# Sequence layer with a scan in blocks: where the decay from a token to later blocks is made (sums first, exponential in token order, one transposition), on one core

## The chip, the core and the metric

One core of a Trainium2 chip. The metric is the device time of one execution in microseconds (us). Of the core's engines five matter here: TensorE (matrix products and transpositions, results to PSUM), VectorE, ScalarE and GpSimd (element by element), and the queues that issue transfers. In the profile they are PE (PEld for its weight loads), DVE, ACT, POOL and SP.

## The reference

Two sequences of 2048 tokens with 256 features. A normalisation, then a state space layer with 512 inner channels and 16 states, then a second normalisation and a feed-forward layer with butterfly weights, each added to its input. The change concerns the scan:

```
delta = softplus(x_dbl[..., 0]);  B = x_dbl[..., 1:17];  C = x_dbl[..., 17:33]
A = -exp(A_log)
step:  h = h * exp(delta_t * A) + x_t * (delta_t * B_t)
       y_t = einsum('dn,n->d', h, C_t)
```

## The kernel before

Time runs in four tiles of 512 tokens (index k), each in four groups of 128 tokens (index c), each group in eight blocks of 16 (index j). Both sequences ("batch" b = 0 and 1) go through a tile one after the other. The scan is written as products: inside a block token by token ("diagonal"), from a token to later blocks of its group ("off diagonal"), and from group to group through a state of 16 x 512.

For the off-diagonal part each token's B needs its decay up to the start of every later block. The kernel before makes it so. `softplus` (L1380) gives `delta` per token and `dB` = delta times B, with tokens on the partitions. GpSimd's `weigh_gaps` (L560) spreads rate times `before_block` times delta over 128 columns (8 blocks x 16 states) for each group: `gap_w`. TensorE's `gap_products` (L768) multiplies it with the matrix `after`, which sums over later tokens and transposes at once. ScalarE's `exp_gaps` (L1099) takes the exponential out of PSUM into `b_hat`. Beside that, GpSimd's `mask_b` (L542) spreads `dB` in token order (`bd_tok`), TensorE transposes it (`decayed_b`, L877), and VectorE's `weigh_b` (L1437) multiplies the two. `off_diagonal` (L810) then forms the product of `b_hat` and `c_hat`.

Each engine runs its list of instructions in a fixed order, written out by hand in `first_half` and `second_half` (the names occur once for each engine); semaphores tie the engines together. PSUM tiles are dealt out in a ring of three wide and three small banks by `WIDE_ORDER` and `SMALL_ORDER` (L60 to L75): a use waits until the use three places earlier in its list has been read. The second half of one tile and the first half of the next stand in one loop; the first half of tile 1 stands ahead of it, with the preparation of the weights between its steps.

The order around the change, in the first half, batch 0: VectorE runs `softplus`, a convolution (three steps, `convolve`, L1342), `take_sums` (L1406), a convolution, `weigh` (L1424), `weigh_b`, a convolution, two `diagonal_times_c` (L1464), a convolution, `sum_diagonal`, `assemble`, `advance_state` and four `gate`s (L1488). GpSimd runs `place_c`, `weigh_gaps`, `mask_b`, `diagonal_gaps` (L550), `place_c_block` (L568) and `diagonal_times_b` (L577). ScalarE runs `exp_sums`, `copy_z`, `exp_gaps`, `copy_z`, `exp_diagonal`, `take_c_start`, `take_c_block`, `copy_z`, `copy_first_state`, then `silu_x` of batch 1 (behind a table load). TensorE runs `step_sums` (L756), a projection, `decayed_b`, a projection, `decayed_c_start`, `spread_c`, `decayed_c_block`, a projection, `off_diagonal`, `state_inputs` (L787), `x_projection` of batch 1 (L731) and `ssm_output` (L820), which writes the tiles that the gates read.

In batch 1 VectorE's order is `softplus`, `first_residual`, `second_stats`, `take_sums`, `weigh`, `second_normalise` (L1512, four `tensor_scalar` steps of L1255), `weigh_b`, `low_parts`; GpSimd's is `mask_b`, `rstd_of`, `diagonal_gaps`, `place_c_block`, and, from the second half, `residual_with_bias` (L582). TensorE transposes the normalised tile (`ln2T`, L709), then `c_start` and `cbd`, then runs `state_inputs` and the feed-forward products.

Of the kernel before, what the change touches and what calls it, by code (L numbers as in the profile page):

```python
# [30 lines left out]
ALU = mybir.AluOpType  # L31
# [3 lines left out]
P = 128  # L35
# [4 lines left out]
NS = 16  # L40
# [81 lines left out]
def bass_preln_ssm_butterfly_ffn(  # L122
# [4 lines left out]
    with ctx:  # L127
# [40 lines left out]
        rate_before = sb("rate_before", [P, NB, NS])  # L168
# [15 lines left out]
        delta = sb("delta", [P, GR])  # L184
# [64 lines left out]
        def mark_read(ins, name, i, b):  # L249
# [21 lines left out]
        gap_w_ready = Signal(sem("gap_w_ready"), 1)  # L271
        c_placed = Signal(sem("c_placed"), 1)
        bd_ready = Signal(sem("bd_ready"), 1)
        sums_ready = Signal(sem("sums_ready"), 1)
# [21 lines left out]
                     gaps_ready, diag_summed, c_start_ready, c_block_ready, b_end_ready, states_ready, gated, hid_ready]  # L296
        by_scalar = [halo_moved, xi_copied, xc_ready, z_ready, exp_ready, decays_ready, group_decay_ready, diag_exp,
                     first_state, halo_saved, hid_high]
        by_pool = [rstd1, rstd2, c_placed, gap_w_ready, bd_ready, diag_gaps, cbd_ready, diag_times_b, x1b_ready]
# [177 lines left out]
        def _(pool):  # L477
# [64 lines left out]
            def mask_b(k, b):  # L542
# [6 lines left out]
                                   ALU.mult).then_inc(bd_ready.handle, 1)  # L549
# [9 lines left out]

            def weigh_gaps(k, b):  # L560

                pool.wait_ge(dB_ready.handle, dB_ready.value(k, b, 1))
                written(pool, k, "gap", 0, b, ago=1)
                pool.tensor_tensor(gap_w[:, :, :, :].rearrange("p c j n -> p c (j n)"),
                                   rate_before[:, :, :].rearrange(flat).unsqueeze(1).to_broadcast([P, GR, P]),
                                   delta[:, :].unsqueeze(2).to_broadcast([P, GR, P]), ALU.mult)\
                    .then_inc(gap_w_ready.handle, 1)
# [21 lines left out]
            def first_half(k):  # L589
                place_c(k, 0)  # L590
                weigh_gaps(k, 0)
                mask_b(k, 0)
                diagonal_gaps(k, 0)
                place_c_block(k, 0)
                diagonal_times_b(k, 0)
                place_c(k, 1)
                weigh_gaps(k, 1)
                mask_b(k, 1)
                rstd_of(k, 0, BATCH, var2, rstd2)
                diagonal_gaps(k, 1)  # L600
                place_c_block(k, 1)

# [18 lines left out]
        def _(pe):  # L621
# [134 lines left out]
            def step_sums(k, b):  # L756
# [5 lines left out]
                for n, mask in enumerate((upto, block_upto, after)):  # L762
                    pe.matmul(bank[:, n * GR:(n + 1) * GR], mask[:, :], delta[:, :], start=True, stop=True)
                pe.matmul(bank[:, 12:13], dA[:, :, :].rearrange(flat), ones[:, 0:1], start=True, stop=True)
                mark_written(pe.matmul(bank[:, 16:16 + GR * BL], in_block[:, :], d_place[:, :, :].rearrange(flat),
                                       start=True, stop=True), "sums", 0, b)

            def gap_products(k, b):  # L768

                bank = tile_of("gap", 0, b)  # L770
                free(pe, k, "gap", 0, b)
                pe.wait_ge(gap_w_ready.handle, gap_w_ready.value(k, b, 1))
                for c in range(GR):
                    last = pe.matmul(bank[:, c * P:(c + 1) * P], gap_w[:, c, :, :].rearrange(flat), after[:, :],
                                     start=True, stop=True)
# [888 lines left out]
```

## Time and profile before

| | |
|---|---|
| time, median of 3 runs | 631.44 us (630.95 to 631.99) |
| the profiled execution | 632.72 us, its span 630.8 us |
| TensorE busy (PE) | 560.5 us, 89% of the span |
| VectorE busy (DVE) | 443.5 us, 70% |
| ScalarE busy (ACT) | 303.1 us, 48% |
| GpSimd busy (POOL) | 123.9 us, 20% |
| granted TensorE clock, mean | 0.951 of 2.4 GHz |

A busy share is an average over stages with different limits, and TensorE's busy time counts products that overlap in its pipeline. What a stage waits for is read from its own stretch: from the waits in brackets in the timeline, and from the chain of work that ended last.

### The profile page before, as it was taken

The numbers are of one execution on the slowest core, as the hardware profiler recorded it, in microseconds if no ns is written. First come the engines' busy times: TensorE is split into PE (matmuls) and PEld (weight loads), VectorE is DVE, ScalarE is ACT, GpSimd is POOL, SyncE is SP. The second block draws the span as 40 slices with busy tenths as digits, with TensorE's granted clock in tenths as the row PEclk, the third lists the DMA queues.
The fourth block names the chain that finished last, engine by engine and source line by source line (L and its number), as shares of the span: only waits on it lengthen the run. The fifth ranks groups of instructions, "written<-read, shape, count | busy, mean of one in ns | idle before, by whom it ended". The sixth has DMA issues, their size and how long they took to land.

```text
span 630.8 us, 8980 instructions
## 1 busy us (share of the span) xinstructions
PE 560.5 (89%) x2996; PEld 436.9 (69%) x2996; DVE 443.5 (70%) x883; ACT 303.1 (48%) x511; POOL 123.9 (20%) x104
## 2 busy tenths in 40 slices
PE   4989776679999997979999989979999988979996
PEld 3747345647899773747899665847899664848895
DVE  5748868876556789877556699887555699977432
ACT  3655739146055766044144866054254865162252
POOL 4213100240012032250021042250020041340010
PEclk9988876899999999979999998979999999979999
DMA  8332020010010100010000000000100000000000
GB/s 239 4 22 4 0 66 2 1 35 2 3 64 2 34 1 2 0 34 0 33 33 0 33 0 0 0 33 0 33 33 0 33 0 0 0 0 2 0 34 34
DMA packets 33067, 12.88 MB, mean 20 GB/s; under 512 B 22003, under 2 KB 32499, under 8 KB 33044
## 3 DMA queue, kind: packets, MB, share of 16 engines
q1 hardware_dynamic: 31444, 9.96, 7.3%
q10 hardware_dynamic: 1600, 2.62, 1.2%
q8 instruction: 13, 0.21, 0.2%
q14 instruction: 10, 0.08, 0.0%
HBM read 8.39 MB, written 4.19 MB: 20 GB/s over the span
## 4 chain that ended last, share of the span: by engine, by line
PE 58%; DVE 23%; ACT 8%; issue 7%; DMA 2%; POOL 1%; DVEq 0%; ACTq 0%; POOLq 0%
PE acc L869 14%; PE wide L858 12%; PE wide L727 8%; DVE xc L1346 6%; PE wide L847 4%; PE wide L829 4%; PE wide L836 4%; PE wide L736 3%; DVE x1b_xn L1255 2%; PE small L717 2%; DVE soft L1385 2%; PE acc L656 1%; PE small L806 1%; DVE diag_sum L1475 1%; PE small L784 1%
## 5 line engine op out<-in xcount | busy, mean ns | idle before, releaser
L1031 ACT ACTIVATE hid_f<-wide,bias_up 128x512 f32<-128x512 f32 x64 | 44.0, 687 | 139.3 <-PE acc L869 127.4
L1346 DVE SCALAR_TENSOR_TENSOR xc<-xi,taps,xc 128x512 f32<-128x512 f32 x96 | 91.0, 958 | 6.5 <-ACT xc L1060 4.2
L1363 DVE TENSOR_TENSOR hid_low<-hid_f,hid_high 128x512 fp32r<-128x512 f32 x64 | 44.3, 692 | 68.8 <-ACT hid_high L1132 68.2
L869 PE MATMUL acc<-w_down_high,hid_high 128*128 128x256 f32 x256 | 73.9, 289 | 1.5 <-DVE hid_low L1363 1.5
L869 PE MATMUL acc<-w_down_low,hid_high 128*128 128x256 f32 x256 | 71.8, 281 | 0.0
L869 PE MATMUL acc<-w_down_high,hid_low 128*128 128x256 f32 x256 | 71.7, 280 | 0.0
L847 PE MATMUL wide<-w_out,yg 128*128 128x256 f32 x256 | 56.9, 380 | 0.0
L537 POOL TENSOR_TENSOR c_place<-xd,row_in_block 128x1024 f32<-128x1024 f32 x8 | 15.5, 1938 | 208.8 <-DVE xd L1374 208.8
L727 PE MATMUL wide<-xnT_high,w_in_high 128*128 128x512 f32 x128 | 54.9, 429 | 0.0
L858 PE MATMUL wide<-xnT_high,w_up_high 128*128 128x512 f32 x128 | 53.4, 417 | 0.0
L869 PEld LDWEIGHTS acc<-w_down_high,hid_high 128*128 128x128 f32 x256 | 48.2, 188 | 6.6 <-DVE hid_low L1363 4.5
L847 PEld LDWEIGHTS wide<-w_out,yg 128*128 128x128 f32 x256 | 48.0, 190 | 6.6
L727 PE MATMUL wide<-xnT_low,w_in_high 128*128 128x512 f32 x128 | 52.2, 408 | 0.0
L727 PE MATMUL wide<-xnT_high,w_in_low 128*128 128x512 f32 x128 | 52.0, 406 | 0.0
L858 PE MATMUL wide<-xnT_high,w_up_low 128*128 128x512 f32 x128 | 50.3, 393 | 0.0
L858 PE MATMUL wide<-xnT_low,w_up_high 128*128 128x512 f32 x128 | 50.1, 391 | 0.0
L869 PEld LDWEIGHTS acc<-w_down_low,hid_high 128*128 128x128 f32 x256 | 48.3, 189 | 1.8
L501 POOL TENSOR_TENSOR rstd<-var_eps,minus_half 128x4 f32<-128x4 f32 x16 | 19.0, 1186 | 154.5 <-DVE var_eps L1250 154.2
L869 PEld LDWEIGHTS acc<-w_down_high,hid_low 128*128 128x128 f32 x256 | 48.4, 189 | 0.0
L829 PEld LDWEIGHTS wide<-m_mat,x_tok 128*128 128x128 f32 x256 | 33.6, 209 | 18.2 <-ACT xdT L1031 10.3
L829 PE MATMUL wide<-m_mat,x_tok 128*128 128x128 f32 x256 | 35.1, 296 | 10.0 <-ACT xdT L1031 9.1
L1132 ACT ACTIVATE hid_high<-hid_f 128x512 fp32r<-128x512 f32 x64 | 40.6, 634 | 2.0
(184 smaller groups left out, 1136.4 us busy)
## 6 DMA issues: line engine op xcount, KB each, us to landing
x_in<-in_L_attn_x_dram SPq DMA_DIRECT2D x8, 512.0 KB, 3.6
out_dram<-x1b_xn SPq DMA_DIRECT2D x8, 512.0 KB, 2.9
xc<-in_L_attn_in_proj_w_dram ACTq DMA_DIRECT2D x2, 512.0 KB, 6.6
xc<-in_L_ffn_W_exp_dram ACTq DMA_DIRECT2D x1, 1024.0 KB, 9.3
low_w<-in_L_ffn_W_con_dram SPq DMA_DIRECT2D x1, 1024.0 KB, 5.6
raw_out<-n_L_attn_out_proj_w_dram ACTq DMA_DIRECT2D x1, 512.0 KB, 10.3
low_w<-in_L_ffn_up_weights_dram SPq DMA_DIRECT2D x14, 4.0 KB
low_w<-_L_ffn_down_weights_dram SPq DMA_DIRECT2D x14, 4.0 KB
```

What stands on the lines that cost most here:

```text
L501: pool.tensor_tensor(rstd[:, slot, :], var_eps[:, slot, :], minus_half[:, :], ALU.pow)\
L727: last = pe.matmul(bank[:, :], w_in[w][:, m, e * P:(e + 1) * P], xnT[x][:, m, :], start=n == 0, stop=n == MB * len(PASSES) - 1)
L736: last = pe.matmul(bank[0:XD, :], w_x[:, g, :], xc[b][:, g, :], start=g == 0, stop=g == CB - 1)
L829: pe.matmul(bank[:, c * P:(c + 1) * P], x_tok[:, c, g * P:(g + 1) * P], m_mat[:, c * P:(c + 1) * P], start=c == 0, stop=False, skip_group_ ...
L836: mark_written(pe.matmul(tile_of("y", g, b)[:, :], state[b][:, g * P:(g + 1) * P], c_startT[:, :], start=False, stop=True, skip_group_chec ...
L847: last = pe.matmul(bank[:, q * DM:(q + 1) * DM], yg[:, g, c * P:(c + 1) * P], w_out[:, g, :], start=g == 0, stop=g == CB - 1)
L858: last = pe.matmul(bank[:, :], w_up[w][:, m, j * P:(j + 1) * P], xnT[x][:, m, :], start=n == 0, stop=n == MB * len(PASSES) - 1)
L869: last = pe.matmul(acc[:, c, :], hid[h][:, j % HRING, c * P:(c + 1) * P], w_down[w][:, j, 0:DM], start=j == 0 and c % 2 == 0 and n == 0, s ...
L1031: ins = act.activation(out_ap, in_ap, how.pop("func"), **how)
L1132: act.activation(hid[0][:, j % HRING, :], hid_f32[:, j % HRING, :], ACT.Copy).then_inc(hid_high.handle, 1)
L1346: ins = dve.scalar_tensor_tensor(xc[b][:, e, :], xi[:, e, tap:tap + TILE], taps[:, e, tap:tap + 1], xc[b][:, e, :], ALU.mult, ALU.add)
L1363: dve.tensor_tensor(hid[1][:, j % HRING, :], hid_f32[:, j % HRING, :], hid[0][:, j % HRING, :].bitcast(F32), ALU.subtract).then_inc(hid_re ...
```

## The change

The decay of a token to the start of a later block is now made in token order. `softplus` writes, beside `delta`, the products `steps_before` of `before_block` and `delta` (8 for each group), next to it in one tile `steps_at`. `step_sums` multiplies `after` with all 36 columns of it, so that the sums of the steps come per token and block. `take_sums` multiplies these by the rates on VectorE into `gap_w`, ScalarE takes the exponential in place, and GpSimd multiplies it into `bd_tok`. One transposition by TensorE then yields the finished B, and ScalarE copies it to `b_hat`. The product `gap_products`, its bank, GpSimd's `weigh_gaps`, VectorE's `weigh_b` and the constant `rate_before` are gone. `decayed_b` stands later in TensorE's order, and `bd` later in the order of the small banks.

```diff
-    + [("xtok", c, 0) for c in range(GR)] + [(name, 0, 0) for name in ("xdtok", "sums", "gap", "bd")]
-    + [("ct", 0, 0), ("cb", 0, 0), ("cb", 1, 0)] + [(name, 0, 0) for name in ("cbd", "moff", "u")]
-    + [("xtok", c, 1) for c in range(GR)] + [(name, 0, 1) for name in ("xdtok", "sums", "gap", "bd")]
+    + [("xtok", c, 0) for c in range(GR)] + [(name, 0, 0) for name in ("xdtok", "sums")]
+    + [("ct", 0, 0), ("cb", 0, 0), ("cb", 1, 0)] + [(name, 0, 0) for name in ("cbd", "bd", "moff", "u")]
+    + [("xtok", c, 1) for c in range(GR)] + [(name, 0, 1) for name in ("xdtok", "sums")]
     + [("ln2T", m, 0) for m in range(MB)]
-    + [("ct", 0, 1), ("cbd", 0, 1), ("u", 0, 1), ("cb", 0, 1), ("cb", 1, 1), ("moff", 0, 1)]
+    + [("ct", 0, 1), ("cbd", 0, 1), ("bd", 0, 1), ("u", 0, 1), ("cb", 0, 1), ("cb", 1, 1), ("moff", 0, 1)]
...
# GpSimd
+            def weigh_b(k, b):
+                pool.wait_ge(gap_decays.handle, gap_decays.value(k, b, 1))
+                pool.wait_ge(b_masked.handle, b_masked.value(k, b, 1))
+                pool.tensor_tensor(bd_tok[:, :, :, :], bd_tok[:, :, :, :], gap_w[:, :, :, :], ALU.mult)\
+                    .then_inc(bd_ready.handle, 1)
...
                 place_c(k, 0)
-                weigh_gaps(k, 0)
                 mask_b(k, 0)
                 diagonal_gaps(k, 0)
                 place_c_block(k, 0)
+                weigh_b(k, 0)
                 diagonal_times_b(k, 0)
                 place_c(k, 1)
-                weigh_gaps(k, 1)
                 mask_b(k, 1)
                 rstd_of(k, 0, BATCH, var2, rstd2)
                 diagonal_gaps(k, 1)
                 place_c_block(k, 1)
+                weigh_b(k, 1)
...
# TensorE
                 for n, mask in enumerate((upto, block_upto, after)):
-                    pe.matmul(bank[:, n * GR:(n + 1) * GR], mask[:, :], delta[:, :], start=True, stop=True)
+                    steps = steps_at[:, :] if mask is after else delta
+                    pe.matmul(bank[:, n * GR:n * GR + steps.shape[1]], mask[:, :], steps, start=True, stop=True)
...
             def decayed_b(k, b):
-                gap_products(k, b)
                 transpose_groups(k, "bd", b, lambda c: bd_tok[:, c, :, :].rearrange(flat), bd_ready)
...
                 in_projection(k, 1, 4)
-                decayed_b(k, 0)
...
                 in_projection(k, 1, 6)
+                decayed_b(k, 0)
                 off_diagonal(k, 0)
...
-                decayed_b(k, 1)
                 in_projection(k, 1, 7)
                 transposes(k, "ln2T", 0, xn2, norm2)
                 decayed_c_start(k, 1)
                 decayed_c_block(k, 1)
+                decayed_b(k, 1)
                 state_inputs(k, 1)
...
# ScalarE
             def exp_gaps(k, b):
+                act.wait_ge(gap_exponents.handle, gap_exponents.value(k, b, 1))
+                whole = gap_w[:, :, :, :].rearrange("p c j n -> p (c j n)")
+                act.activation(whole, whole, ACT.Exp).then_inc(gap_decays.handle, 1)
+
+            def take_b_hat(k, b):
                 written(act, k, "moff", 0, b, ago=1)
-                take(k, "gap", 0, b, b_hat[:, :], tile_of("gap", 0, b)[:, :], func=ACT.Exp)
+                take(k, "bd", 0, b, b_hat[:, :], tile_of("bd", 0, b)[:, :])
...
                 take_c_block(k, 0)
+                take_b_hat(k, 0)
                 copy_z(k, 1, 6)
...
                 take_c_block(k, 1)
+                take_b_hat(k, 1)
                 copy_first_state(k, 1)
...
# VectorE
-                link_setup(dve.tensor_tensor(rate_before[:, :, :], before_block[:, :].unsqueeze(2).to_broadcast([P, NB, NS]),
-                                       rates[:, :].unsqueeze(1).to_broadcast([P, NB, NS]), ALU.mult))
...
+                dve.tensor_tensor(steps_before, before_block[:, :].unsqueeze(1).to_broadcast([P, GR, NB]),
+                                  delta.unsqueeze(2).to_broadcast([P, GR, NB]), ALU.mult)
...
+                dve.wait_ge(bd_ready.handle, bd_ready.value(k, b, 1, ago=1))
+                dve.tensor_tensor(gap_w[:, :, :, :].rearrange("p c j n -> p (c j) n"),
+                                  bank[:, 12:12 + GR * NB].unsqueeze(2).to_broadcast([P, GR * NB, NS]),
+                                  rates[:, :].unsqueeze(1).to_broadcast([P, GR * NB, NS]), ALU.mult)\
+                    .then_inc(gap_exponents.handle, 1)
...
                 weigh(k, 0)
-                weigh_b(k, 0)
...
                 second_normalise(k, 0)
-                weigh_b(k, 1)
```

## Rows read from the trace of the kernel before

**Rows 1.** The page, chain that ended last: shares of the span by engine.
```profile
PE 58%; DVE 23%; ACT 8%; issue 7%; DMA 2%; POOL 1%; DVEq 0%; ACTq 0%; POOLq 0%
```

**Rows 2.** Timeline, tile 2, batch 0: start, us, engine, line, operation [wait, releaser].
```profile
239.00 0.63 PE L784 MATMUL small<-ident,c_start 128*128 128x128 f32 x4 [3.00 <-DVE c_start L1429]
...
243.22 0.60 ACT L1031 ACTIVATE z<-wide 128x512 f32<-128x512 f32 x1 [0.80 <-PE wide L727]
...
244.34 1.28 ACT L1069 ACT_TABLE_LOAD   x1
...
244.65 1.15 PE L816 MATMUL small<-c_hat,b_hat 128*128 128x128 f32 x8 [1.47 <-DVE diag L1470]
...
245.64 2.38 ACT L1069 ACTIVATE xc<-xc 128x512 f32<-128x512 f32 x4
```

**Rows 3.** Timeline, batch 1: the second normalisation in tiles 1 and 2.
```profile
134.14 4.31 DVE L1255 TENSOR_SCALAR x1b_xn<-x,mean_var,rstd 128x256 f32<-128x256 f32 x4
...
271.43 1.99 POOL L555 TENSOR_TENSOR diag<-gaps,rates 128x1024 f32<-128x1024 f32 x1
271.57 5.77 DVE L1255 TENSOR_SCALAR x1b_xn<-x,mean_var,rstd 128x256 f32<-128x256 f32 x4
...
273.38 1.14 POOL L573 TENSOR_TENSOR cbd_tok<-c_block,in_block 128x512 f32<-128x512 f32 x1
273.71 0.30 PE L717 MATMUL small<-ident,x1b_xn 128*128 128x128 f32 x1 [1.90 <-DVE x1b_xn L1255]
274.48 2.38 POOL L586 TENSOR_TENSOR x1b_xn<-x,bias_out 128x1024 f32<-128x1024 f32 x1
```

**Rows 4.** Chain that ended last in order of time: start, us, what.
```profile
84.71 5.56 DMA low_w<-in_L_ffn_W_con_dram
...
277.07 1.65 PE small L717 x6
278.72 1.74 PE small L784 x8
```

**Rows 5.** Timeline, tile 2: VectorE and GpSimd from 230 to 246 us, and 280.38.
```profile
230.33 1.04 POOL L564 TENSOR_TENSOR gap_w<-rate_before,delta 128x512 f32<-128x512 f32 x1 [2.86 <-DVE dB L1398]
230.36 3.81 DVE L1346 SCALAR_TENSOR_TENSOR xc<-xi,taps,xc 128x512 f32<-128x512 f32 x3
231.32 1.51 POOL L546 TENSOR_TENSOR bd_tok<-dB,before_block 128x512 f32<-128x512 f32 x1
...
239.04 0.68 DVE L1441 TENSOR_TENSOR b_hat<-b_hat,small 128x512 f32<-128x512 f32 x1
...
239.64 4.29 DVE L1346 SCALAR_TENSOR_TENSOR xc<-xi,taps,xc 128x512 f32<-128x512 f32 x3
240.21 2.38 POOL L579 TENSOR_TENSOR diag<-diag,dB 128x1024 f32<-128x1024 f32 x1
243.84 1.28 DVE L1470 TENSOR_TENSOR diag<-diag,small 128x512 f32<-128x512 f32 x2
245.04 2.32 DVE L1346 SCALAR_TENSOR_TENSOR xc<-xi,taps,xc 128x512 f32<-128x512 f32 x3
...
280.38 1.93 POOL L579 TENSOR_TENSOR diag<-diag,dB 128x1024 f32<-128x1024 f32 x1 [3.52 <-ACT diag L1119]
```

**Rows 6.** First gate of tiles 2 and 3; last, a stretch with its granted clock (PEclk).
```profile
254.41 0.75 DVE L1493 SCALAR_TENSOR_TENSOR yg<-xc,skip,wide 128x512 f32<-128x512 f32 x1 [0.59 <-PE wide L836]
...
378.41 0.68 DVE L1441 TENSOR_TENSOR b_hat<-b_hat,small 128x512 f32<-128x512 f32 x1
...
388.69 3.59 PE L736 MATMUL wide<-xc,w_x 128*33 128x512 f32 x8 [1.35 <-ACT xc L1069]
...
395.27 0.75 DVE L1493 SCALAR_TENSOR_TENSOR yg<-xc,skip,wide 128x512 f32<-128x512 f32 x1 [2.09 <-PE wide L836]
...
378.40:380.40 2.00, 2.00 (x6) 1.48 (x7) 1.96 (x4) 0.60 (x1) 1.88 (x2) 0.50 0.00 0
```

**Rows 7.** Groups of instructions, form by form: the products with `after`.
```profile
L774 PE MATMUL small<-after,gap_w 128*128 128x128 f32 x64 | 8.7, 278 | 1.7 <-DVE w_down_low L1269 1.7
```

More of the change, by code:

```diff
@@ L183, in bass_preln_ssm_butterfly_ffn @@
         soft = sb("soft", [P, 10, GR])
-        delta = sb("delta", [P, GR])
+        steps_at = sb("steps_at", [P, GR + GR * NB])
+        delta, steps_before = steps_at[:, 0:GR], steps_at[:, GR:GR + GR * NB].rearrange("p (c j) -> p c j", j=NB)
         dB = sb("dB", [P, GR, NS])
@@ L270, in bass_preln_ssm_butterfly_ffn @@
         delta_ready = Signal(sem("delta_ready"), 1)
-        gap_w_ready = Signal(sem("gap_w_ready"), 1)
+        gap_exponents = Signal(sem("gap_exponents"), 1)
+        gap_decays = Signal(sem("gap_decays"), 1)
         c_placed = Signal(sem("c_placed"), 1)
         bd_ready = Signal(sem("bd_ready"), 1)
+        b_masked = Signal(sem("b_masked"), 1)
         sums_ready = Signal(sem("sums_ready"), 1)
@@ L295, in bass_preln_ssm_butterfly_ffn @@
         by_vector = [var1, norm1, var2, norm2, convolved, abs_ready, dB_ready, delta_ready, sums_ready,
[L296 to L297 removed]
+                     gaps_ready, gap_exponents, diag_summed, c_start_ready, c_block_ready, b_end_ready, states_ready, gated, hid_ready]
+        by_scalar = [halo_moved, xi_copied, xc_ready, z_ready, exp_ready, decays_ready, group_decay_ready, gap_decays, diag_exp,
                      first_state, halo_saved, hid_high]
[L299 removed]
+        by_pool = [rstd1, rstd2, c_placed, b_masked, bd_ready, diag_gaps, cbd_ready, diag_times_b, x1b_ready]
         def start(eng, signals):
@@ L558, in diagonal_gaps @@
                                    ALU.mult).then_inc(diag_gaps.handle, 1)
[L560 to L567, printed above, removed]
             def place_c_block(k, b):
@@ L762, in step_sums @@
                 for n, mask in enumerate((upto, block_upto, after)):
-                    pe.matmul(bank[:, n * GR:(n + 1) * GR], mask[:, :], delta[:, :], start=True, stop=True)
-                pe.matmul(bank[:, 12:13], dA[:, :, :].rearrange(flat), ones[:, 0:1], start=True, stop=True)
-                mark_written(pe.matmul(bank[:, 16:16 + GR * BL], in_block[:, :], d_place[:, :, :].rearrange(flat),
+                    steps = steps_at[:, :] if mask is after else delta
+                    pe.matmul(bank[:, n * GR:n * GR + steps.shape[1]], mask[:, :], steps, start=True, stop=True)
+                pe.matmul(bank[:, 44:45], dA[:, :, :].rearrange(flat), ones[:, 0:1], start=True, stop=True)
+                mark_written(pe.matmul(bank[:, 48:48 + GR * BL], in_block[:, :], d_place[:, :, :].rearrange(flat),
                                        start=True, stop=True), "sums", 0, b)
[L768 to L775, printed above, removed]
-                mark_written(last, "gap", 0, b)
             def transpose_groups(k, name, b, source, ready):
@@ L1410, in take_sums @@
                 dve.wait_ge(group_decay_ready.handle, group_decay_ready.value(k, b, 1, ago=1))
-                dve.tensor_copy(group_sum[:, :], bank[:, 12:13])
+                dve.tensor_copy(group_sum[:, :], bank[:, 44:45])
                 dve.tensor_tensor(sums_A[:, :, :], bank[:, 0:3 * GR].unsqueeze(2).to_broadcast([P, 3 * GR, NS]),
@@ L1414, in take_sums @@
                     .then_inc(sums_ready.handle, 1)
-                mark_read(dve.tensor_tensor(d_block[:, :, :], bank[:, 16:16 + GR * BL].rearrange("p (c u) -> p c u", u=BL),
+                dve.wait_ge(bd_ready.handle, bd_ready.value(k, b, 1, ago=1))
[3 more added lines that the diff above has]
+                    .then_inc(gap_exponents.handle, 1)
+                mark_read(dve.tensor_tensor(d_block[:, :, :], bank[:, 48:48 + GR * BL].rearrange("p (c u) -> p c u", u=BL),
                                             later_in_block[:, :].unsqueeze(1).to_broadcast([P, GR, BL]), ALU.mult),
@@ L1435, in weigh @@
                     .then_inc(b_end_ready.handle, 1)
-            def weigh_b(k, b):
-                written(dve, k, "bd", 0, b)
-                read(dve, k, "gap", 0, b)
-                mark_read(dve.tensor_tensor(b_hat[:, :], b_hat[:, :], tile_of("bd", 0, b)[:, :], ALU.mult), "bd", 0, b)
             def advance_state(k, b):
```

12 lines of the change are left out of this document (5 added, 7 removed).

## The prediction, made before the change was run

> **What bounds the kernel now.** I read the page's chain first: TensorE holds 58% of what ended last, VectorE 23%, and the two trade places inside every tile [rows 1]. I then followed the chain in order of time, then the timelines of the two stretches where the diff works, and the grouped list for prices. Tiles are numbered 1 to 4; the times below are tile 2's unless said otherwise.
>
> In the first stretch (batch 0, 229 to 255 us) VectorE never rests and TensorE waits for it: 3.00 us for `c_start`, 1.47 us for `diag` [rows 2]. In the second (batch 1, 267 to 287 us) the four `second_normalise` operations take 5.77 us together, and TensorE waits for them piece by piece, 1.90 us for the first alone [rows 3]; the chain then runs through the transposes at 277.07 [rows 4]. After that TensorE is busy nearly without a gap to the next tile, so a delay in either stretch reaches the end.
>
> Two things are to be seen in the rows. First, VectorE's convolution steps and GpSimd's operations take turns. Three steps take 2.32 us with GpSimd idle, but 3.81 and 4.29 us beside it; GpSimd's `diag<-diag,dB` takes 2.38 us beside them and 1.93 where VectorE doesn't disturb it [rows 5, 6]. In `second_normalise` a step ends only when a GpSimd operation does: the first after `diag` (273.42), the second after `cbd_tok` (274.52), the third after `x1b_xn` (276.86), and the fourth, with nothing beside it, by 277.34 [rows 3].
>
> The Trainium skill says the same of the mechanism ("SBUF — State Buffer", Who interferes with whom: VectorE and GpSimd take the shared port pair for a whole instruction and the other one fully blocks). Had they shared the bandwidth instead, both would merely run slower, `diagonal_times_c` below would come at about 244.4 and not 244.7, and the sum would be some 0.8 us less (642.7). The turns in rows 3 and 5 agree with the lock.
>
> Second, tile 3 of this very kernel shows what a late ScalarE costs: TensorE ran at half clock there (0.50, 1.2 GHz), its products came late to ScalarE, `x_projection` waited 1.35 us for `silu_x`, and the first `gate` began 16.86 us after the `b_hat` product (378.41 to 395.27) against 15.37 us in tile 2 (239.04 to 254.41) [rows 6]. A delay of 1.5 us there was not absorbed by VectorE.
>
> **The change, part by part.**
>
> *What goes.* Eight products with `after` for each tile and batch go from TensorE, 64 in all, 8.7 us busy [rows 7]. None is worth anything: in both batches the next TensorE step waits for VectorE (3.00 us, then 1.90 us) [rows 2, 3], so TensorE only waits longer. VectorE's `b_hat` product goes, 0.68 us with the next starting after 0.60 [rows 5]. In batch 0 that is on the path; in batch 1 it stood between the last normalise and a wait for ScalarE, so it gives nothing. Set-up loses one 128x128 VectorE operation, about 0.3 us, on the path of tile 1.
>
> *What comes on VectorE.* The exponents in `take_sums` are 128x512 out of PSUM, no row of before has them; the nearest is the `b_hat` product (same size, one operand in PSUM): 0.61 us, bounds 0.6 and 0.95 (a convolution step waiting its turn; nothing excludes that). `steps_before` is a 128x32 operation, 0.14 us by the starts of the 128x64 ones beside it. The wider product with `after` has 36 columns for 4, and VectorE comes to the sums late in both batches: nothing. Two more new waits are met early: `take_sums` waits for `weigh_b` of the other batch, done some 20 us before, and `exp_gaps` for the exponents; behind it only copies of `z` are queued, for which nobody is waiting yet.
>
> *GpSimd in batch 0.* `gap_w` (1.04 us) leaves the first convolution, which thereby ends about 0.7 us sooner, and that pays for exponents and `steps_before`: `c_start` comes when it came before. `weigh_b` reads two full 128x512 operands; I take 1.05 us from `gap_w`, bounds 1.04 and 1.51 (`bd_tok` in turns) [rows 5]. It stands between `cbd_tok` and `diag<-diag,dB`. With one more turn for the convolution in between (about 0.5 us each), GpSimd finishes `diag` at about 244.6 instead of 242.59. VectorE, which without `b_hat` would be done with convolution 2 at about 242.9, must wait, and `diagonal_times_c` starts at 244.7 instead of 243.84: 0.85 us late.
>
> *The new wait in batch 0.* This is the largest term. By the new bank order the `bd` transposes take the bank of `cb` 0, so they wait for the first `diagonal_times_c`. Before, `off_diagonal` waited for the same event (start 244.65) [rows 2]; now it stands behind three more steps: transposes, ScalarE's copy, then the product. On ScalarE the copy stands ahead of `copy_z`, `copy_first_state`, the table load and `silu_x`, all of which wait with it. The steps: `cb` read at 245.4; four transposes 0.63 (from `c_start`) to 246.1 [rows 2]; `take_b_hat` 0.60 as the copy of `z`, to 246.75; then `copy_z` and `copy_first_state`, 1.12 from the first's start to the table load's, to 247.85; table load 1.28, to 249.1; first `silu_x` 0.62, to 249.75 [rows 2]. TensorE's own path (`off_diagonal` 1.15, the state inputs about as much again) ends at about 249, so ScalarE comes last. `x_projection` starts at 249.8, that is 10.76 us after the old `b_hat` instant, where tile 3 of before had 10.28 (378.41 to 388.69) [rows 6]. Tile 3 had its gate at 16.86; this makes 17.34 against 15.37: 2.0 us late. Tiles 2 and 4 lose 2.0 us each, tile 3, which already had 1.5 of it, 0.5 us. VectorE was at rest for the last of it, so the 0.85 us lies inside the 2.0. In tile 1 `x_projection` leads on to the load of `W_con`, 5.56 us, which stands on the chain [rows 4]; set-up work lies between the steps there, and by the same count I get 1.1 us.
>
> *Batch 1.* Exponents and `steps_before` make the scan 0.75 us late; GpSimd's `diag` starts some 0.6 us late, at 272.0 instead of 271.43 (before, `rstd` ended a little after the scan). Then come `cbd_tok` (1.14), the new `weigh_b` (1.05) and `x1b_xn` (2.38). A fourth GpSimd operation now stands in front of the fourth normalise step: the third step slips in after `weigh_b`, the fourth only after `x1b_xn`, at 278.6 instead of 277.34 [rows 3]. The transposes of `xn2` end 1.2 us late. Behind them stand the four new `bd` transposes: 0.45 us at full clock, 0.87 at the half clock these run at (eight took 1.74) [rows 4]. ScalarE's copy is held by them and holds `copy_first_state`, `silu_z` and the first gelu by as much. I take 0.6: 1.8 us for tiles 2 to 4 each. In tile 1 the normalise took 4.31 us with two GpSimd operations beside it [rows 3]; a third adds 0.95, with the transposes 1.4 us.
>
> **Sum.** Batch 0: 2.0 + 2.0 + 0.5 + 1.1 = 5.6. Batch 1: 3 x 1.8 + 1.4 = 6.8. Set-up: -0.3. Together 12.1 us. The profiled execution took 632.72 us (span 630.8, 1.9 around it): 644.8. The median of the runs shown is 1.3 us (0.2%) below it, so I predict 643.5.
>
> **The rivals.** (1) *Batch 0 absorbs its wait*: `take_b_hat` comes early enough that silu isn't late, for instance if GpSimd gets its turns first and `diag` ends at 243. Then only batch 1 and set-up count: 631.44 + 6.8 - 0.3 = 638. Against it stands tile 3, whose gate came 1.5 us late from such a wait. (2) *The clock falls as well*: TensorE's idle time before `c_start` grows from 3.00 to some 4.3 us (products and transposes are gone from ahead of it), and it is nearly idle again from 243.2 until the silu. The eight products of `x_projection` take 3.6 us at full clock [rows 6] and would take 3.6 more at half; as the clock comes back on the way I count half of that, 1.8 us. In three tiles: 649. After the same 3.00 us of idling tile 3 of before ran at 0.50 [rows 6], and tile 2 did not (four transposes in 0.63 us [rows 2]), so it can go either way. (3) *Faster*: TensorE is freed of products, and if in every tile it, and not VectorE, were the late one behind them, the 64 products would come back: 8.7 us busy as the bound, 623; half of it, 627. It decides from the point at which the waits behind the products (3.00 and 1.90 us) shrink to nothing, for instance if VectorE's convolutions beside GpSimd lost their turns no more. I see nothing in the rows that does this. (4) *Nothing measurable*: late ScalarE and late normalise each have slack I can't see: within 0.2% of 631.4. That the change doesn't do what it says would also land here: the old product is replaced by work of the same sizes on other engines.
>
> **How the numbers follow.** Forecast 0.62; (1) 0.12; (2) 0.17; (3) 0.05; (4) 0.04. Less than 0.2% (1.3 us) can hardly be told from no change in a measurement of this kernel. Slower: 0.62 + 0.12 + 0.17 = 0.91; same 0.04; faster 0.05. The range goes from (1), 637.5, to (2) with `weigh_b` at its upper bound in part, 650; what is outside is the two small cases and the tails.
>
> **What would show it.** In the profile after: `diagonal_times_c` at half a microsecond to one late and directly behind GpSimd's `diag`; TensorE waiting for `b_hat` ahead of `off_diagonal`, and `x_projection` for `silu_x` in all of tiles 2 to 4; first `gate` some 17.3 us after the end of `weigh`, where tile 2 of before had 15.4; `second_normalise` of about 6.3 us, its third step ending with `weigh_b`, its fourth with `x1b_xn`. If `x_projection` starts without a wait for ScalarE, the largest term is wrong; if the normalise is no longer than 5.8 us, that of batch 1 is; a tile at half clock in `x_projection` means rival 2.

## The result, and the profile after

The changed kernel took 648.61 us (median of 4 runs, 647.15 to 650.57) beside 631.2 us for the kernel before: ratio 1.0273, 95% interval 1.0249 to 1.0297, 17.4 us slower. Its profiled execution took 647.48 us with a span of 645.7, 14.9 more than the span of before. VectorE is busy for 445.3 us (69%), GpSimd for 128.6 (20%), TensorE for 555.6 (86%); the granted clock is 0.944 on the mean, where before had 0.951. Of the chain that ended last, TensorE and VectorE now hold less and GpSimd 5% where it held 1% [rows 1]:

```profile
PE 56%; DVE 18%; issue 10%; ACT 8%; POOL 5%; DMA 2%; DVEq 0%; ACTq 0%; POOLq 0%
```

Where the 14.9 us came, by landmarks in the two timelines (batch 0: from the first copy of the halo to the copy of `xd` of batch 1; batch 1: from there to the next tile's halo):

| tile | batch 0, us | batch 1, us |
|---|---|---|
| 1, with set-up | -2.3 | +5.0 |
| 2 | +2.15 | +2.29 |
| 3 | +0.64 | +2.56 |
| 4 | +2.11 | +2.45 |

Batch 0 of tile 2 after, all engines (start, us, engine, line, operation, in brackets the idle time before and who ended it); it answers to [rows 2, 5, 6]:

```profile
241.28 0.22 DVE L1430 TENSOR_TENSOR c_start<-xd,decays 128x64 f32<-128x64 f32 x1
...
243.35 1.71 POOL L557 TENSOR_TENSOR bd_tok<-bd_tok,gap_w 128x512 f32<-128x512 f32 x1
...
245.03 2.38 POOL L579 TENSOR_TENSOR diag<-diag,dB 128x1024 f32<-128x1024 f32 x1
...
247.53 1.28 DVE L1465 TENSOR_TENSOR diag<-diag,small 128x512 f32<-128x512 f32 x2 [1.92 <-POOL diag L579]
...
248.27 0.66 PE L775 MATMUL small<-ident,bd_tok 128*128 128x128 f32 x4 [0.75 <-DVE diag L1465]
...
249.03 0.60 ACT L1021 ACTIVATE b_hat<-small 128x512 f32<-128x512 f32 x1 [2.27 <-PE small L775]
...
249.75 1.15 PE L807 MATMUL small<-c_hat,b_hat 128*128 128x128 f32 x8 [0.82 <-ACT b_hat L1021]
...
252.69 3.59 PE L736 MATMUL wide<-xc,w_x 128*33 128x512 f32 x8 [0.81 <-ACT xc L1059]
...
259.17 0.75 DVE L1488 SCALAR_TENSOR_TENSOR yg<-xc,skip,wide 128x512 f32<-128x512 f32 x1 [1.64 <-PE wide L827]
```

GpSimd's `weigh_b` (243.35) stands between `cbd_tok` and `diag`; VectorE waits 1.92 us for `diag`, the `bd` transposes 0.75 for VectorE, `off_diagonal` 0.82 for ScalarE's `b_hat`, `x_projection` 0.81 for `silu_x`. The first gate starts 17.89 us after `c_start`, 15.77 in the kernel before (238.64 to 254.41 [rows 6]).

Batch 1 of tile 2 after, from the exponents to the transposes of the normalised tile; it answers to [rows 3]:

```profile
275.66 0.68 DVE L1412 TENSOR_TENSOR gap_w<-small,rates 128x512 f32<-128x512 f32 x1
...
276.88 1.95 POOL L564 TENSOR_TENSOR diag<-gaps,rates 128x1024 f32<-128x1024 f32 x1 [0.47 <-DVE gaps L1421]
...
276.97 1.95 DVE L1435 TENSOR_TENSOR b_end<-dB,decays 128x64 f32<-128x64 f32 x1
278.80 1.09 POOL L573 TENSOR_TENSOR cbd_tok<-c_block,in_block 128x512 f32<-128x512 f32 x1
278.84 5.14 DVE L1252 TENSOR_SCALAR x1b_xn<-x,mean_var,rstd 128x256 f32<-128x256 f32 x4
279.86 1.30 POOL L557 TENSOR_TENSOR bd_tok<-bd_tok,gap_w 128x512 f32<-128x512 f32 x1
...
281.12 2.39 POOL L586 TENSOR_TENSOR x1b_xn<-x,bias_out 128x1024 f32<-128x1024 f32 x1
...
283.71 1.65 PE L717 MATMUL small<-ident,x1b_xn 128*128 128x128 f32 x6 [1.88 <-DVE x1b_xn L1252]
```

The exponents (0.68 us) make the scan and all behind it late. `b_end`, an operation of 128x64 elements that took 0.22 us before, now starts 0.09 us behind GpSimd's `diag` and ends with it: 1.95 us. The four normalise steps follow: three of them end with GpSimd's next three operations, the fourth runs alone and ends at 283.98, 0.47 us after the residual. The groups of instructions, form by form (busy time, mean ns of one), have it for all eight of these operations, two in each tile: 1.95 us in batch 1 of tiles 2 to 4, 0.22 in the other five. In the kernel before their mean was 221 ns:

```profile
L1435 DVE TENSOR_TENSOR b_end<-dB,decays 128x64 f32<-128x64 f32 x8 | 6.9, 867 | 0.0
```

### The profile page after: what moved, and what is told of

Read it like the earlier page. It is cut to its first block, busy times and chain, and to the rows that moved or that the text cites. A ratio compares the mean times of both kernels' runs of the same rounds, so it can differ in the third digit from the quotient of the medians.

```text
span 645.7 us, 8898 instructions
## 1 busy us (share of the span) xinstructions
PE 555.6 (86%) x2932; PEld 430.3 (67%) x2932; DVE 445.3 (69%) x890; ACT 307.3 (48%) x519; POOL 128.6 (20%) x104
## 3 DMA queue, kind: packets, MB, share of 16 engines
HBM read 8.39 MB, written 4.19 MB: 19 GB/s over the span
## 4 chain that ended last, share of the span: by engine, by line
PE 56%; DVE 18%; issue 10%; ACT 8%; POOL 5%; DMA 2%; DVEq 0%; ACTq 0%; POOLq 0%
PE acc L860 14%; PE wide L849 12%; PE wide L727 5%; PE wide L820 5%; PE wide L838 4%; PE wide L827 4%; PE wide L736 4%; DVE x1b_xn L1252 3%; DVE xc L1341 2%; PE small L717 2%; DVE soft L1380 2%; POOL diag L579 1%; PE small L775 1%; PE small L745 1%; DVE soft L1386 1%
## 5 line engine op out<-in xcount | busy, mean ns | idle before, releaser
L1341 DVE SCALAR_TENSOR_TENSOR xc<-xi,taps,xc 128x512 f32<-128x512 f32 x96 | 85.9, 906 | 6.5 <-ACT xc L1050 4.2
L727 PE MATMUL wide<-xnT_high,w_in_high 128*128 128x512 f32 x128 | 53.3, 416 | 1.7 <-DVE w_down_low L1266 1.6
```

Of the source, the lines that this page charges most:

```text
L727: last = pe.matmul(bank[:, :], w_in[w][:, m, e * P:(e + 1) * P], xnT[x][:, m, :], start=n == 0, stop=n == MB * len(PASSES) - 1)
L1341: ins = dve.scalar_tensor_tensor(xc[b][:, e, :], xi[:, e, tap:tap + TILE], taps[:, e, tap:tap + 1], xc[b][:, e, :], ALU.mult, ALU.add)
```

## The experiments

All times are medians; "before" was run beside each group of experiments and stood between 630.75 and 632.25 us.

**Does the place of GpSimd's multiplication in batch 1 matter?** The first reading was that it stands ahead of the residual, and so ahead of the last normalise step.

```diff
                 place_c_block(k, 1)
-                weigh_b(k, 1)
...
                 residual_with_bias(k, 0)
+                weigh_b(k, 1)
```

> The changed kernel with one step of GpSimd moved: in batch 1 weigh_b runs behind residual_with_bias and not ahead of it. Changed kernel: 648.6 us. Theory (the second normalisation ends with GpSimd's residual, and weigh_b stands ahead of that): the normalisation ends 1.1 to 1.3 us sooner in each of four tiles, 643.5 to 644.5. Rival, the clock (longer rests put TensorE at half clock more often): no more than chance, 647 to 650. Rival, the exponents on VectorE are the loss: 648.6.

Measured: 649.11 us, ratio 1.028 (1.0237 to 1.0323). No gain; tile 2 is as long as before the edit (143.80 us). The timeline of this kernel, batch 1 of tile 2, says why:

```profile
276.54 1.95 DVE L1435 TENSOR_TENSOR b_end<-dB,decays 128x64 f32<-128x64 f32 x1
278.37 1.09 POOL L573 TENSOR_TENSOR cbd_tok<-c_block,in_block 128x512 f32<-128x512 f32 x1
278.41 5.14 DVE L1252 TENSOR_SCALAR x1b_xn<-x,mean_var,rstd 128x256 f32<-128x256 f32 x4
279.43 2.38 POOL L586 TENSOR_TENSOR x1b_xn<-x,bias_out 128x1024 f32<-128x1024 f32 x1
...
281.77 1.31 POOL L557 TENSOR_TENSOR bd_tok<-bd_tok,gap_w 128x512 f32<-128x512 f32 x1
```

The four steps again last 5.14 us: now the second waits for the residual and the third for the multiplication. This change of order is of no account, and the first reading fell. The next run asks about the number of operations: it takes the multiplication out of the row.

```diff
                 place_c_block(k, 1)
-                weigh_b(k, 1)
...
                 residual_with_bias(k, 0)
+                pool.wait_ge(norm2.handle, norm2.value(k, 0, GR))
+                weigh_b(k, 1)
```

> The changed kernel, with GpSimd's multiplication of batch 1 placed behind the residual with bias and made to wait until the second normalisation is done, so that no VectorE step can fall behind it. If the normalisation's steps each wait for one GpSimd operation and the multiplication is one operation too many in that row (theory), one of four waits goes, 1.1 to 1.3 us for each tile: 643.5 to 645 us against 648.6, with the transposes of the normalised tile that much earlier. If the time in batch 1 is set by ScalarE's additional copy, or by GpSimd's total work wherever it stands (rival), nothing is gained: 648 to 649 us, as when the multiplication was only moved behind the residual.

Measured: 646.46 us, ratio 1.0245 (1.0224 to 1.0267); 2.2 us less than the changed kernel, below what the theory asked. In the timeline of the same stretch the theory holds: the normalise takes 4.19 us in place of 5.14.

```profile
279.97 4.19 DVE L1253 TENSOR_SCALAR x1b_xn<-x,mean_var,rstd 128x256 f32<-128x256 f32 x4
...
284.39 1.27 POOL L557 TENSOR_TENSOR bd_tok<-bd_tok,gap_w 128x512 f32<-128x512 f32 x1 [1.02 <-DVE x1b_xn L1253]
...
288.03 1.53 PE L787 MATMUL small<-x_tok,b_end 128*16 128x512 f32 x8
...
289.84 0.73 DVE L1450 SCALAR_TENSOR_TENSOR state<-state_end,group_decay,small 16x512 f32<-16x512 f32 x1 [2.94 <-PE small L787]
```

But 0.66 us of it is lost on the way to VectorE's state step (5.68 us behind the normalise, 5.02 in the changed kernel), which waits 2.94 us for the state inputs. These take 1.53 us for 1.05. The granted clock (last column but two, by stretches of the time) is still at 0.50, that is 1.2 GHz, just ahead of them and 0.65 on the mean while they run; in the changed kernel (last row) it was 0.94 from 286.5 to 288 us, and the state inputs started at 287.48:

```profile
287.00:288.00 1.00, 1.00 (x6) 0.70 (x4) 0.00 (x0) 1.00 (x3) 0.80 (x1) 0.50 0.00 0
288.00:289.50 1.50, 1.50 (x10) 0.15 (x9) 0.00 (x0) 1.44 (x4) 1.13 (x1) 0.65 0.00 0
...
286.50:288.00 1.50, 1.46 (x15) 0.72 (x13) 0.22 (x1) 1.50 (x4) 0.98 (x1) 0.94 0.00 0
```

Tiles 2 to 4 as a whole gained 0.85, 0.94 and 0.75 us each.

**The exponents.** Once more the same operation, its result into a tile that is overwritten later:

```diff
+                dve.tensor_tensor(m_mat[:, :].rearrange("p (a n) -> p a n", n=NS),
+                                  bank[:, 12:12 + GR * NB]..., rates..., ALU.mult)
```

> The changed kernel with the 128x512 exponents on VectorE written a second time in each take_sums (into a tile that is free there), 8 more operations of 0.61 us; the result is unchanged. Rival, the exponents are the loss: each costs what it lasts, 8 x 0.6 = 4.9 us, 653.5. Theory: in batch 0 VectorE waits 1.6 us at the first gate, and most of the 0.6 goes into that; in batch 1 the scan and GpSimd's chain move by 0.6 in each tile: 3 x 0.6 to 4 x 0.6, with a part of batch 0, 650.5 to 652.

Measured: 654.06 us, ratio 1.0354 (1.0318 to 1.039). In the profile batch 0 of tiles 2 to 4 grew by 0.58 to 0.62 us and batch 1's stretch up to `c_start` by 0.60 in each: nearly all of their 0.68 us, in both batches. So the rival held (653.5), and the theory, by which batch 0 would hide most of it (650.5 to 652), fell: the exponents cost about what they last. (The profiled execution was the fastest of its four, 651.09 us, 3.6 above that of the changed kernel; the rest of the 5.45 us between the medians isn't taken apart.) Then the exponents were moved behind the scan (batch 0) and behind the weighed products (batch 1):

```diff
...
                 weigh(k, 1)
+                exponents(k, 1)
                 second_normalise(k, 0)
```

> The changed kernel, with VectorE's exponents behind the scan in batch 0 and behind the three weighed products in batch 1. If what makes the small product for the block's end last 1.95 us for 0.22 is that the exponents push it behind the start of GpSimd's diagonal (theory), it is short again, the first normalise step takes its place behind the diagonal, and the normalisation ends 0.4 to 0.6 us sooner in each tile: 646 to 647.2 us against 648.6. If the exponents' own 0.68 us is what counts, wherever it stands (rival), nothing changes: 648.2 to 649.

Measured: 647.82 us, ratio 1.0249 (1.0218 to 1.0281), between what the two asked. The step that was named did not happen, as the timeline of batch 1 of tile 2 shows:

```profile
279.23 1.93 POOL L564 TENSOR_TENSOR diag<-gaps,rates 128x1024 f32<-128x1024 f32 x1
279.30 1.94 DVE L1436 TENSOR_TENSOR b_end<-dB,decays 128x64 f32<-128x64 f32 x1
281.12 1.09 POOL L573 TENSOR_TENSOR cbd_tok<-c_block,in_block 128x512 f32<-128x512 f32 x1
281.17 0.68 DVE L1421 TENSOR_TENSOR gap_w<-small,rates 128x512 f32<-128x512 f32 x1
```

`diag` is earlier too, since GpSimd's `rstd` now ends last before it, and `b_end` still starts 0.07 us behind it and lasts 1.94 us. In the kernel before it started 0.01 us ahead of `diag` (271.43 [rows 3]):

```profile
271.42 0.22 DVE L1434 TENSOR_TENSOR b_end<-dB,decays 128x64 f32<-128x64 f32 x1
```

So 0.1 us decides over 1.7. The exponents at 281.17, with one operand in PSUM, took their 0.68 us beside `cbd_tok`. The Trainium skill ("SBUF — State Buffer", Who interferes with whom) makes that difference: an operation of VectorE with at most one input in SBUF stays clear of the lock, unless it runs in a two-port mode; one with two waits for a GpSimd operation that reads SBUF. The rows of the exponents and of `b_end` agree; the normalise steps, with one tensor in SBUF, wait, so they would be of the two-port kind.

**GpSimd's operation by itself, in the kernel before.** One more 128x512 operation in each batch (`dB` times `before_block` into `gap_w`, behind its last reader), where the change has its multiplication.

```diff
...
                 place_c_block(k, 0)
+                spare_op(k, 0)
...
                 place_c_block(k, 1)
+                spare_op(k, 1)
```

> The kernel before, with one additional GpSimd operation of 128x512 in each batch, placed where the changed kernel has its multiplication (behind the spread of C's block); its result is not used, nothing else is changed. If GpSimd's operation by itself takes its turn from VectorE (theory), it costs 0.9 to 1.3 us in each batch of a tile, except perhaps in tile 3's batch 0: 637.5 to 641 us against 631.8. If the changed kernel loses by its new waits and its later order alone, and the operation is covered (rival): 632 to 633.5 us.

Measured: 636.55 us, ratio 1.009 (1.0069 to 1.0111): 5.6 us, somewhat less than the theory asked. Its timeline, batch 0 of tile 2:

```profile
239.92 4.96 DVE L1355 SCALAR_TENSOR_TENSOR xc<-xi,taps,xc 128x512 f32<-128x512 f32 x3
...
240.49 1.50 POOL L553 TENSOR_TENSOR gap_w<-dB,before_block 128x512 f32<-128x512 f32 x1
...
244.81 1.27 DVE L1479 TENSOR_TENSOR diag<-diag,small 128x512 f32<-128x512 f32 x2
```

In batch 0 `diagonal_times_c` comes 0.69 us later after `c_start` than before (5.89 by 5.20); in batch 1 the normalise takes 6.51 us for 5.77 [rows 3]. The fourth step before had run alone, for 0.48 us; now it stands behind the residual, so 0.4 of the 1.1 us is hidden. The 5.6 us are about a third of the change's 17.4. They are a price before what the change gives back: it takes another GpSimd operation of this size away, `weigh_gaps`, which here stayed.

**Batch 0: the queue on ScalarE.** First its copy of `b_hat` behind the copies that `silu_x` waits for:

```diff
-                take_b_hat(k, 0)
                 copy_z(k, 1, 6)
                 copy_first_state(k, 0)
+                take_b_hat(k, 0)
```

> The changed kernel with ScalarE's take_b_hat of batch 0 moved behind copy_z and copy_first_state, all else as it is. Theory (the copy holds up what stands behind it on ScalarE, and silu_x is late): both copies are done while ScalarE waits, x_projection starts 1.1 us sooner in tiles 2 to 4, first gate as well: 645 to 646. Rival, VectorE is what is late (GpSimd's longer chain ahead of diagonal_times_c): the gates don't move, 648.6. Rival clock: 647 to 650.

Measured: 645.75 us, ratio 1.0221 (1.0186 to 1.0256). Batch 0 is 0.83 to 0.87 us shorter in tiles 2 to 4, `x_projection` no longer waits for `silu_x`, and the first gate comes 17.04 us after `c_start` for 17.89. So the copy's place in ScalarE's list is worth some 0.85 us; the rest of the 2.1 us lies ahead of it. Then the whole chain early: `weigh_b` ahead of `place_c_block`, the transposes of B ahead of C's, the copy behind `exp_diagonal`, and `bd` first in the order of the small banks.

```diff
+                weigh_b(k, 0)
                 place_c_block(k, 0)
-                weigh_b(k, 0)
...
+                decayed_b(k, 0)
                 decayed_c_start(k, 0)
```

> The changed kernel with batch 0 ordered otherwise: GpSimd's weigh_b ahead of place_c_block, where it rested 1.8 us; bd the first of the small banks behind sums, its transposes ahead of c_start's, ScalarE's copy right behind exp_diagonal. Nothing waits for the read of cb then. Theory (the new wait of batch 0 is the bank order and the copy's place): the first gate comes back to within 0.5 to 1 us of where it was after weigh in the kernel before, 1.2 to 1.6 us a tile in tiles 2 to 4, 644 to 645. Rival clock: 647 to 650. Rival exponents: no gain.

Measured: 646.02 us, ratio 1.0215 (1.018 to 1.0251): somewhat less gain than expected. The new wait is gone, and its price has moved (timeline, batch 0 of tile 2):

```profile
239.60 4.73 DVE L1341 SCALAR_TENSOR_TENSOR xc<-xi,taps,xc 128x512 f32<-128x512 f32 x3
...
242.07 1.71 POOL L557 TENSOR_TENSOR bd_tok<-bd_tok,gap_w 128x512 f32<-128x512 f32 x1
...
244.26 0.21 DVE L1430 TENSOR_TENSOR c_start<-xd,decays 128x64 f32<-128x64 f32 x1
...
260.04 0.75 DVE L1488 SCALAR_TENSOR_TENSOR yg<-xc,skip,wide 128x512 f32<-128x512 f32 x1 [0.98 <-PE wide L827]
```

From `c_start` to the gate it is 15.78 us, as in the kernel before (16.2 and 16.3 in tiles 3 and 4). But `weigh_b` now stands beside the convolution ahead of `c_start`, which takes 4.73 us for 3.84, and `c_start` comes that much later. In both places GpSimd's 128x512 operation stands beside VectorE's two-operand steps, and VectorE pays for it: 0.9 us here, 0.7 in the run on the kernel before.

**All repairs together.** The early chain, the multiplication behind the second normalisation, the late exponents, and batch 1's `b_hat` copy taken from ScalarE's list into VectorE's:

```diff
...
-                take_b_hat(k, 1)
...
                 low_parts(k, "ln2T", 0)
+                take_b_hat(k, 1)
```

> The changed kernel with all that helped or should help together: in batch 0 the transposition of B ahead of that of C, with GpSimd's multiplication and ScalarE's copy brought forward; in batch 1 the multiplication behind the second normalisation, the exponents behind the weighed products, and the copy on VectorE at its rest after the low parts. If the parts add up (theory): 2.6 us in batch 0 by the earlier run, 4 to 5 in batch 1 by multiplication and exponents, 1 to 2 by the copy: 638 to 641.5 us against 648.6, still slower than the kernel before by its exponents and GpSimd's time in batch 0. If the end is set by something that these share, such as the lower clock (rival), the sum is not reached: 643.5 to 646.

Measured: 639.08 us, ratio 1.0137 (1.0116 to 1.0157). That is the time forecast, but not by the parts: the three edits that were run by themselves gained 2.6, 2.2 and 0.8 us against the changed kernel, 5.5 together, and all four gained 9.5. The other 4 us belong to the copy, which no run has by itself, or to the edits acting together; that stays open. 8 us remain.

**The row of turns, in both kernels.** If the normalise steps wait for GpSimd, the cure is to let GpSimd wait. One line, in the kernel before and in the changed one:

```diff
                 rstd_of(k, 0, BATCH, var2, rstd2)
+                pool.wait_ge(norm2.handle, norm2.value(k, 0, GR))
                 diagonal_gaps(k, 1)
                 place_c_block(k, 1)
```

> The kernel before with one edit: in batch 1 GpSimd waits until the second normalisation is done before it makes the diagonal, spreads C's block and adds the residual's bias. If each normalise step lasts as long as the GpSimd operation that it falls behind (theory), the four steps, 5.77 us together in tile 2 and 4.31 in tile 1, shrink to 1.2 to 1.5 us; the transposes come 3 to 4 us sooner in tiles 2 to 4, 2 to 3 in tile 1, less what the later diagonal gives back on ScalarE: 616 to 622 us against 631.2. If the stretch is then bound by ScalarE's exponential of the diagonal or by the transposition of C's block, which now come late (rival), little is left: 627 to 632.

Measured: 620.72 us, ratio 0.9843 (0.9824 to 0.9861). It beats both kernels. In its timeline the four steps, 5.77 us together [rows 3], take 1.38, and the transposes run right behind them:

```profile
269.59 1.38 DVE L1256 TENSOR_SCALAR x1b_xn<-x,mean_var,rstd 128x256 f32<-128x256 f32 x4
...
270.15 1.64 PE L718 MATMUL small<-ident,x1b_xn 128*128 128x128 f32 x8 [0.32 <-DVE x1b_xn L1256]
...
271.05 1.93 POOL L555 TENSOR_TENSOR diag<-gaps,rates 128x1024 f32<-128x1024 f32 x1 [1.57 <-DVE x1b_xn L1256]
...
274.18 0.89 PE L785 MATMUL small<-ident,cbd_tok 128*128 128x128 f32 x4 [1.90 <-POOL cbd_tok L573]
```

Not all of the 4.4 us comes out: the transposes of C's block now wait 1.90 us for GpSimd, and from `c_start` to VectorE's state step the tiles 2 to 4 gained 3.3, 2.8 and 3.0 us.

> The changed kernel with the same single edit: in batch 1 GpSimd waits for the second normalisation before the diagonal, the spread of C's block, its multiplication and the residual. If the change's cost in batch 1 is GpSimd's additional operation in the row of turns (theory), this kernel gains more than the kernel before does by the same edit, by 1.2 to 1.8 us for each tile, and stands 8 to 12 us behind it instead of 17: 627 to 632 us. If the cost in batch 1 is the additional exponents and copy (rival), both gain the same and the distance stays 15 to 17: 632 to 637.

Measured: 635.71 us, ratio 1.0085 (1.0066 to 1.0104), 15.0 us behind the kernel before with the same edit. That is the rival's distance: of the 17.4 us only about 2.4 hung on the row of turns of batch 1. By the landmarks of the first table, batch 1 of tiles 2 to 4 costs 1.5 us each with the line in both kernels, for 2.3 to 2.6 without it. The timeline, batch 1 of tile 2:

```profile
276.07 0.22 DVE L1436 TENSOR_TENSOR b_end<-dB,decays 128x64 f32<-128x64 f32 x1
276.21 1.38 DVE L1253 TENSOR_SCALAR x1b_xn<-x,mean_var,rstd 128x256 f32<-128x256 f32 x4
...
282.02 1.09 PE L776 MATMUL small<-ident,bd_tok 128*128 128x128 f32 x4
...
283.04 1.82 PE L787 MATMUL small<-x_tok,b_end 128*16 128x512 f32 x8
...
285.13 0.74 DVE L1450 SCALAR_TENSOR_TENSOR state<-state_end,group_decay,small 16x512 f32<-16x512 f32 x1 [4.92 <-PE small L787]
```

With GpSimd held back `b_end` takes its 0.22 us again, in the changed kernel too, so its 1.95 us were GpSimd's `diag`. The normalise is as short as in the kernel before with the same line (1.38 us), and the price stands one step further: cbd, then the multiplication, then four more transposes (282.02) ahead of the state inputs, and VectorE's state step waits 4.92 us. From `c_start` to that step it is 9.31 us; with the edit in the kernel before 8.02. The last run has the line together with all the repairs.

> The changed kernel with all repairs: the early transposition of B in batch 0, the exponents behind the weighed products, the copy of batch 1 on VectorE, and GpSimd's four operations of batch 1 behind the second normalisation. If the parts add up as in the run with all repairs before (639.1 us, there with the multiplication alone moved behind), the three more operations moved behind give another 2 to 3.5 us for each tile: 626 to 632 us, about the kernel before as it stands, and 7 to 12 us behind the kernel before with the same edit, which is the change's own price in batch 0 and in VectorE's exponents. If the gain from the normalisation goes back to ScalarE (rival): 636 to 639.

Measured: 630.41 us (624.87 to 632.78), ratio 0.9986 (0.9961 to 1.001): as fast as the kernel before as it stands, 9.7 us behind the kernel before with the same edit.

**The clock.** TensorE's waits filled with repeated products:

```diff
+                for again in range({(1, 5): 3, (1, 7): 4}.get((b, e), 1)):
                     for n, (m, w, x) in enumerate(...):
                         last = pe.matmul(...)
```

> The changed kernel with TensorE kept at work in its two long waits: the projection of column group 5 of batch 1 is computed three times over and that of group 7 four times, the same products with the same result, about 2.8 and 4.2 us more of them in each tile, inside waits of 4.2 and 4.9 us. If TensorE's half clock in the stretches behind these waits is a price of the change of its own (theory: the rival of the falling clock), the granted clock of those stretches comes back to 1.00, the transposes behind the second normalisation take 0.6 us for each four instead of 0.9 to 1.1, and the time falls by 0.8 to 1.3 us in each tile: 643.5 to 645.5 us, with less spread. If the half clock lies beside ScalarE's chain and VectorE's waits (rival), the time stays at 647.5 to 649.5 although the clock rises; if the products keep other steps waiting, it is more than that.

Measured: 655.8 us, ratio 1.0366 (1.0343 to 1.0389), slower than theory and rival asked; the expectation had left that open for products that keep other steps waiting. In batch 0 it was something else. The half clock didn't go, it moved (tile 2; the last row is a stretch with its granted clock):

```profile
252.50 0.66 PE L776 MATMUL small<-ident,bd_tok 128*128 128x128 f32 x4 [2.46 <-DVE diag L1466]
...
253.98 2.07 PE L808 MATMUL small<-c_hat,b_hat 128*128 128x128 f32 x8 [0.82 <-ACT b_hat L1022]
...
257.82 4.71 PE L737 MATMUL wide<-xc,w_x 128*33 128x512 f32 x8
...
265.41 0.75 DVE L1489 SCALAR_TENSOR_TENSOR yg<-xc,skip,wide 128x512 f32<-128x512 f32 x1 [3.68 <-PE wide L828]
...
254.00:256.00 2.00, 2.00 (x11) 1.78 (x13) 1.97 (x3) 1.98 (x3) 0.00 (x0) 0.50 0.05 12
```

The transposes of `c_start` run at full clock (0.63 us), and the four of C's block behind them (0.60 for 0.81 in the changed kernel). But then TensorE rests 2.46 us for VectorE, and the eight products of `off_diagonal` take 2.07 us for 1.15, those of `x_projection` 4.71 for 3.59: the granted clock from 254 to 260 us is 0.50. The first gate stands 19.93 us after `c_start`, 2.0 more than in the changed kernel (18.66 and 19.82 in tiles 3 and 4). Tile 1 also lost 4.2 us, which wasn't taken apart. Behind the second wait it was the same: 0.50 from 291 to 293 us, the transposes of `c_start` and of C's block at 1.06 and 1.12 us.

## Why the prediction was right, and where its sizes were off

The sign, the places and most prices held: 643.5 us was forecast, 648.6 measured. Of the 5.1 us, 2.7 are in the sum (14.8 between the two profiled executions, for 12.1). The other 2.4 lie between profiled executions and medians: that of before stood 1.3 us above its median, which the forecast took off, and that of after 1.1 below.

*Batch 0* was right in nearly every step. `c_start` comes 8.70 us after `dB` in both kernels, as said: the shorter convolution pays for the exponents. `diagonal_times_c` was to be 0.85 late: 1.05. `x_projection` was to start 10.76 us after the old `b_hat` instant, which is 11.16 after `c_start`: 11.41. The gate at 17.34, or 17.74 after `c_start`: 17.89. Tiles 2, 3 and 4 lost 2.15, 0.64 and 2.11 us for 2.0, 0.5 and 2.0. The explanation was half the matter: it put the delay on the queue of transposes and copy. The runs show that the copy's place is worth some 0.85. With the whole chain early the wait behind `c_start` is gone in tile 2, but `c_start` itself comes 0.9 us later beside GpSimd's operation.

*Batch 1* was mis-sized: 1.8 us for each tile, measured 2.3 to 2.6. The step that failed is "the third step slips in after `weigh_b`, the fourth only after `x1b_xn`": a fifth VectorE operation, `b_end`, fell into the row and took the first turn, so that the fourth step ran alone behind the residual. The prediction had seen that `diag` and the scan move by 0.6 and 0.75 us, but not that `b_end` stood 0.01 us ahead of `diag`. That is 0.5 us a tile (the normalise ends 1.7 us later against the last statistics, for 1.2). The row "`second_normalise` of about 6.3 us" came out as 5.14 for the same reason: 7.01 with `b_end`. By the prediction's own sign (no longer than 5.8 us) the term would be wrong; its lateness was there, but in `b_end`. The 0.6 us for transposes and copy held (0.6 to 0.9 remain), and the run with GpSimd behind the normalisation shows that they take the place of the turns where those are gone.

*Tile 1* was 2.2 us by the sum and 2.7 in the profile, but by other parts: 1.1 - 0.3 for batch 0 with set-up was -2.3, and 1.4 for batch 1 was 5.0. That the two nearly meet is luck. The second eight weight products in its batch 1 ran at half clock after the change, as the timeline has it (after, then before):

```profile
129.18 3.78 PE L679 MATMUL acc<-x1b_xn,paths 128*128 128x256 f32 x8 [1.29 <-DVE w_down_low L1266]
...
130.47 1.99 PE L679 MATMUL acc<-x1b_xn,paths 128*128 128x256 f32 x8 [1.64 <-DVE w_down_low L1269]
```

The granted clock after is 0.50 from 125 to 133 us; ScalarE and VectorE, which take the weights from them, came 1.8 us late. Another 0.85 us went where `d_place`, 0.22 us before, took 1.07 behind GpSimd's `bd_tok`. In set-up it went the other way: from 75 to 90 us the granted clock was 0.89, before 0.73, and the part up to batch 1 was 2.3 us shorter.

*The clock* (rival 2) did not decide batch 0: in tiles 2 to 4 the fall came earlier than the rival put it (0.50 to 0.52 from 242.5 to 245.8 us of tile 2, 1.00 by `x_projection`), where TensorE had time. What such a fall costs where it meets `off_diagonal` and `x_projection` the filled waits showed: 2.0 us in tile 2, near the rival's 1.8. How much of the 17.4 us is clock stays open: the one run that was to take it away moved it. Within one kernel the time goes with it: the kernel with all repairs and the waiting GpSimd took 624.87 us at a mean of 0.960 and 632.78 at 0.943. Rival 1 (batch 0 absorbs) and rival 3 (products come back) are excluded by the first table and by TensorE's busy time, which fell by 4.9 us while its waits grew.

## What to carry to other kernels

When VectorE waits step by step, see which GpSimd operation each step ends with, and count the operations in the row: an operation that moves to GpSimd is not off the path if VectorE works from SBUF at that time. Here the cure was to hold GpSimd back until the critical steps were through, not to reorder it: that one wait was worth 10 us to the kernel before and 13 to the changed one, where all other repairs together were worth 9.5. Before an operation is made late by some tenths, look for small ones that stand just ahead of another engine's long one.

## What the hardware showed that was not expected

An operation of 0.22 us lasted 1.95 us because it started 0.09 us behind a GpSimd operation of 1.95 us; so it went in tiles 2, 3 and 4, and with GpSimd held back it took 0.22 us again. And more work on TensorE in its waits made later products slower: with 2.8 us of products added ahead of `c_start` the granted clock held there, but was 0.50 from 254 to 260 us, where the changed kernel has 1.00.
